# Values in three blocks per group in the first cross attention, and rotated halves formed from one projection in the second self attention

## Chip, cores and metric

The kernel runs on one core of one Trainium2 chip. The metric is the device time of one execution in microseconds (us); smaller is better. An execution is one launch that runs the whole two-layer decoder.

## The reference, cut to what matters

Two decoder layers, each of self attention, cross attention and a feed-forward part, with a layer norm after each. The change touches two of the six parts. The first is layer 0's cross attention, with 2048 queries, 1601 keys and 16 heads of 64:

```python
q = (x @ w_q).reshape(B, SQ, N_HEADS, D_HEAD)
k = (cond @ w_k).reshape(B, SKV, N_HEADS, D_HEAD)
v = (cond @ w_v).reshape(B, SKV, N_HEADS, D_HEAD)
attn = softmax(einsum('bqhd,bkhd->bhqk', q, k) * scale)
out = einsum('bhqk,bkhd->bqhd', attn, v).reshape(B, SQ, N_HEADS * D_HEAD)
return out @ w_out + b_out
```

The second is layer 1's self attention, causal, with 2 heads of 128. Of each head's 128 features the first 64 are rotated by position and the others stay as they are:

```python
even, odd = split(rot, 2, axis=-1)          # 32 features each
r_even = even * cos - odd * sin
r_odd = even * sin + odd * cos
return concatenate([r_even, r_odd, skip], axis=-1)
```

## The kernel before

The parts of the decoder run one after another. Within a part each engine has its own written-out list of instructions, in an order set at build time, and semaphores tie the lists together. An engine never takes its list out of order.

**The first cross attention** (`l0_cross_heads`) works in 32 groups: 8 pairs of heads by 4 tiles of 512 queries. A group has 13 steps, `kt` 0 to 12, one for each 128 keys. In a step TensorE computes the scores of both heads, with the keys on the partitions (`scores`, L867: eight matmuls on 64 rows, so that the two heads lie in the two halves of the array), ScalarE takes the exponential (`exponentials`, L1032) into one of `NP` buffers `pr` (two of them lie in `o_nat`), GpSimd adds it to a running sum (L783, L779), and TensorE multiplies it with the values (`values`, L882: four matmuls of 128 rows by 64 columns for a step). Beside it runs work for later groups. 32 maxima per group, for the group after next or thereabouts: TensorE computes a piece of 400 scores of one head (L823, also on 64 rows), and VectorE reduces it (L921); after the last of a group VectorE takes the least of the pieces (L928), TensorE turns it (L829, "shift"), VectorE copies it (L936), and a DMA puts it in place. Then the projections `q` and `k`, the sum of the exponentials over partitions (`sum`, L835), the output projection (`out`, L845).

These side units share three banks of PSUM, `pM`, in turn. The unit with number n may start on TensorE when the unit n-3 has been emptied: a maximum by VectorE's reduction, `out` by VectorE's addition (L971), `q` and `k` by VectorE's subtraction (L915) after a copy on ScalarE (L1011), `sum` by ScalarE (L1018). VectorE also makes four reciprocals per group (L943, after the maxima of steps 5 to 8) and the normalised output (L950, after those of step 9). `units_in(g, kt)` says which units a step has, 2 or 3 maxima and then the others. `values` run at the end of steps 0, 1, 3, 5, 7, 9 and 11, for one or two steps at a time.

**The second self attention** (`l1_self_attention`) works in 8 items x: 4 tiles of 512 positions by 2 heads. Each item needs q and k rotated. The rotation's swapped halves come from a second projection with columns swapped in the weights (`qs`, `ks`), so that there are four projections per item (L1735, four matmuls each). VectorE multiplies the straight one with cos (L1878), the swapped one with sin (L1887) and adds (L1891); ScalarE rounds the sum to its high part (L2017), and VectorE subtracts for the low part (L1870). Again units share three banks. `project(x + 2)` is laid out during item x: its first two units, then `shift` of item x + 1 (L1771, copied by VectorE in L1914), then the rest. The scores of item x + 1 (L1823) wait for that copy. In items 1 and 2 VectorE also normalises rows of the experts' output (L1955 to L1967) before its first unit, and in items 3 and 5 it takes statistics (L1939, L1941) there.

Of the kernel before, what the change touches and what calls it, by code (L numbers as in the profile page):

```python
# [13 lines left out]
P = 128  # L14
T = 2048
# [595 lines left out]
def l0_cross_heads(nc, A, G, sems):  # L611
# [9 lines left out]
    NP = 4  # L621
# [38 lines left out]
    last = [("out", GROUPS - 2, 1), ("sum", GROUPS - 1), ("out", GROUPS - 1, 0), ("out", GROUPS - 1, 1)]  # L660
# [4 lines left out]
    with ExitStack() as ctx:  # L665
# [11 lines left out]
        unit_rows = m.sb("x0unit", [P, P], F32R)  # L677
        kept = G.o_nat[:, :, :].rearrange("p c n -> p (c n)").bitcast(F32).rearrange("p (b a q) -> p b a q", b=2, a=2)
        pr = [kept[:, 0, :, :], kept[:, 1, :, :]] + [m.sb(f"x0pr{i}", [P, 2, QG])[:, :, :] for i in range(2)]
# [5 lines left out]
        rc = m.sb("x0rc", [P, QG])  # L685
        oc = m.sb("x0oc", [P, QG])
# [38 lines left out]
        with nc.Block() as block:  # L725
            @block.sync
            def _(sp):
# [22 lines left out]
                sp.wait_ge(s_set, 4)  # L750
# [8 lines left out]
            def _(pool):  # L759
                for i in range(2):  # L760
                    nc.gpsimd.memset(sh[i][:, :].bitcast(F32), 0.0).then_inc(s_set, 1)
                nc.gpsimd.memset(unit_rows[:, :].bitcast(F32), 0.0).then_inc(s_set, 1)
                pool.wait_ge(s_set, 3)
                nc.gpsimd.memset(unit_rows[0:1, :].bitcast(F32), 1.0).then_inc(s_set, 1)
                pool.wait_ge(s_set, 4)
                nc.gpsimd.memset(unit_rows[64:65, :].bitcast(F32), 1.0).then_inc(s_set, 1)
                pool.wait_ge(s_set, 5)
# [19 lines left out]
            def _(pe_):  # L787
# [98 lines left out]
                pe_.wait_ge(s_set, 5)  # L886
# [12 lines left out]
                values(STEPS - 2)  # L899
                values(STEPS - 1)  # L900
# [4 lines left out]
            def _(dve):  # L905
# [32 lines left out]
                def reciprocals(g, i):  # L938
                    wait_emptied(dve, ("sum", g))
                    if i == 0 and g >= 1:  # L940
                        dve.wait_ge(s_on, g)
                    c = slice(i * P, (i + 1) * P)
                    nc.vector.reciprocal(rc[:, c], dn[:, c]).then_inc(s_rc, 1)  # L943

                def normalise(g):
                    dve.wait_ge(s_rc, 4 * (g + 1))
                    dve.wait_ge(s_oc, g + 1)
                    if g >= 2:
                        wait_filled(dve, ("out", g - 2, 1))
                    nc.vector.tensor_tensor(on[g % 2][:, :], oc[:, :], rc[:, :], ALU.mult).then_inc(s_on, 1)  # L950
# [40 lines left out]
                unit(last[0])  # L991
                for i in range(4):
                    reciprocals(GROUPS - 1, i)
                normalise(GROUPS - 1)
                for name in last[2:]:
                    unit(name)

            @block.scalar
            def _(act):
# [13 lines left out]
                def sums(name):  # L1013
                    g = name[1]
                    wait_filled(act, name)
                    if g >= 1:
                        act.wait_ge(s_rc, 4 * g)
                    emptied(nc.scalar.activation(dn[:, :], bank(name)[:, :], ACT.Copy), name)  # L1018

                def copy_out(g):  # L1020
                    act.wait_ge(s_pv, NK * (g + 1))
                    if g >= 1:
                        act.wait_ge(s_on, g)
                    nc.scalar.activation(oc[:, :], pO[:, :], ACT.Copy).then_inc(s_oc, 1)
# [527 lines left out]
def l1_self_attention(nc, A, G, sems, acc_d):  # L1552
# [50 lines left out]
    with ExitStack() as ctx:  # L1603
        m = Mem(nc, ctx, sems)
        cos, sin = m.sb("a1cos", [P, T]), m.sb("a1sin", [P, T])
        w = [m.sb(f"a1w{h}", [P, DJ, 4, HD]) for h in range(H)]
# [6 lines left out]
        ta, tb = [m.sb(f"a1ta{i}", [P, QG]) for i in range(2)], m.sb("a1tb", [P, QG])  # L1613
# [23 lines left out]
        s_add, s_hi, s_lo = m.sem("a1_rotated"), m.sem("a1_high"), m.sem("a1_low")  # L1637
# [10 lines left out]
        def emptied(ins, name):  # L1648
            ins.then_inc(s_free[number[name] % 3], 1)
# [18 lines left out]
        with nc.Block() as block:  # L1668
# [57 lines left out]
            def _(pe_):  # L1726
                def rotated(name):
                    kind, x = name
                    g, h = x // H, x % H
                    part = {"q": 0, "qs": 1, "k": 2, "ks": 3}[kind]  # L1730
# [72 lines left out]
                def unit(name):  # L1803
                    if number[name] >= 3:
                        pe_.wait_ge(s_free[number[name] % 3], number[name] // 3)
                    {"q": rotated, "qs": rotated, "k": rotated, "ks": rotated, "v": value_rows, "max": maximum,
# [56 lines left out]
            def _(dve):  # L1863
# [9 lines left out]
                def straight(name):  # L1873
# [9 lines left out]
                def swapped(name):  # L1883
                    kind, x = name[0][0], name[1]
                    wait_filled(dve, name)
                    here = slice((x // H) * QG, (x // H + 1) * QG)
                    emptied(nc.vector.tensor_tensor(tb[:, :], bank(name)[:, :], sin[:, here], ALU.mult), name)  # L1887
                    wait_emptied(dve, (kind, x))
                    wait_emptied(dve, name)
                    mine = ta["qk".index(kind)][:, :]  # L1890
                    nc.vector.tensor_tensor(mine, mine, tb[:, :], ALU.add).then_inc(s_add, 1)  # L1891
# [86 lines left out]
                def unit(name):  # L1978
                    if name[0] not in ("v", "x", "z"):
                        {"q": straight, "qs": swapped, "k": straight, "ks": swapped, "max": maximum, "shift": shifts,  # L1980
# [28 lines left out]
            def _(act):  # L2009
                def high(name):  # L2010
                    kind, x = name[0][0], name[1]
# [20 lines left out]
                def unit(name):  # L2032
                    if name[0] in ("qs", "ks"):
# [826 lines left out]
def rotary_tables():  # L2860
# [5 lines left out]
            np.concatenate([-s, s, np.zeros((64, T), np.float32)]))  # L2866


def layout(i):

    ac = np.ascontiguousarray
    swap = np.concatenate([np.arange(32, 64), np.arange(0, 32), np.arange(64, 128)])
# [13 lines left out]
        "a1_w": np.stack([a1["wq"].reshape(D, D), a1["wq"][:, :, swap].reshape(D, D),  # L2886
                          a1["wk"].reshape(D, D), a1["wk"][:, :, swap].reshape(D, D)]),
# [28 lines left out]
```

## Time and profile before

| | us |
|---|---|
| median of 3 executions | 3599.84 (3599.75 to 3606.65) |
| profiled execution, its own time | 3592.38 |
| its span in the profile | 3590.6 |
| its granted TensorE clock | 0.952 of full speed |

The profiled execution's own time is 1.8 us more than its span. The profile shows the busy time of each engine (PE is TensorE, PEld its weight loads, DVE VectorE, ACT ScalarE, POOL GpSimd), and gives times in us from the span's start. A matmul's record is longer than the time it holds the array, since matmuls overlap; what it holds is read from the distance between starts.

### The profile page before, as it was taken

The numbers are of one execution on the slowest core, as the hardware profiler recorded it, in microseconds if no ns is written. First come the engines' busy times: TensorE is split into PE (matmuls) and PEld (weight loads), VectorE is DVE, ScalarE is ACT, GpSimd is POOL, SyncE is SP. The second block draws the span as 40 slices with busy tenths as digits, with TensorE's granted clock in tenths as the row PEclk, the third lists the DMA queues.
The fourth block names the chain that finished last, engine by engine and source line by source line (L and its number), as shares of the span: only waits on it lengthen the run. The fifth ranks groups of instructions, "written<-read, shape, count | busy, mean of one in ns | idle before, by whom it ended". The sixth has DMA issues, their size and how long they took to land. (4 is left out here: it accounts for less than half of the span.)

```text
span 3590.6 us, 60640 instructions
## 1 busy us (share of the span) xinstructions
PE 3201.4 (89%) x22601; PEld 1809.7 (50%) x22601; DVE 2355.7 (66%) x5271; ACT 1721.9 (48%) x2086; POOL 1711.3 (48%) x1145
## 2 busy tenths in 40 slices
PE   6899999989999999999999817689979989999787
PEld 3666666644555555555555407655544333333346
DVE  3999999945656656656656481264427878888528
ACT  1788888833444344444344322222224656666641
POOL 2888888824767777777778702212350000000012
PEclk9999999999999999999999958889977999999999
DMA  2000000020000000000000066500021111111001
GB/s 71 25 2 2 2 2 2 2 53 1 4 1 3 4 1 4 1 4 1 4 1 1 1 197 202 151 13 1 1 42 17 17 17 17 17 17 17 18 14 36
DMA packets 62572, 88.14 MB, mean 25 GB/s; under 512 B 9458, under 2 KB 52339, under 8 KB 61427
## 3 DMA queue, kind: packets, MB, share of 16 engines
q1 hardware_dynamic: 59250, 80.27, 9.2%
q0 software_dynamic: 3072, 4.34, 0.7%
q8 instruction: 182, 2.98, 0.4%
q14 instruction: 68, 0.55, 0.0%
HBM read 61.28 MB, written 8.54 MB: 19 GB/s over the span
## 5 line engine op out<-in xcount | busy, mean ns | idle before, releaser
L921 DVE TENSOR_REDUCE x0hm<-x0pM 128x1 f32<-128x400 f32 (+1 forms) x1024 | 520.2, 561 | 379.7 <-PE x0pM L823 379.7
L402 POOL TENSOR_SCALAR rows<-rows,mb 128x1024 bf16<-128x1024 bf16 x512 | 567.4, 1119 | 131.2 <-DVE mb L354 131.2
L348 DVE TENSOR_SCALAR_CACHE_REDUCE rows<-pS 128x1024 bf16<-128x1024 f32 x512 | 616.4, 1205 | 19.0 <-PE pS L297 19.0
L413 ACT ACTIVATE prT<-pP 128x1024 bf16<-128x1024 bf16 x512 | 523.3, 1024 | 134.4 <-PE pP L308 133.9
L1381 DVE TENSOR_REDUCE x1hm<-x1pM 128x1 f32<-128x400 f32 (+1 forms) x1024 | 512.6, 564 | 112.3 <-PE x1pM L1273 112.2
L1500 ACT ACTIVATE x1pr<-x1pST 128x1024 f32<-128x1024 f32 (+1 forms) x416 | 419.2, 1023 | 218.3 <-PE x1pST L1325 208.1
L783 POOL TENSOR_TENSOR x0acc<-x0acc,x0pr 128x1024 f32<-128x1024 f32 (+1 forms) x176 | 421.4, 2395 | 111.1 <-ACT x0pr L1032 95.3
L783 POOL TENSOR_TENSOR x0acc<-x0acc,o_nat 128x1024 f32<-128x1024 f32 (+1 forms) x176 | 418.9, 2380 | 71.9 <-ACT o_nat L1032 53.1
L1273 PE MATMUL x1pM<-x1sk,x1sq 64*128 64x400 f32 (+1 forms) x1024 | 361.2, 451 | 58.4 <-DVE x1hm L1381 29.4
L2590 POOL MEMSET f_tri<- 128x128 f32 x1 | 0.2, 209 | 730.2 <-POOLq L1179 730.2
L1032 ACT ACTIVATE o_nat<-x0pST 128x1024 f32<-128x1024 f32 (+1 forms) x208 | 213.0, 1024 | 279.8 <-PE x0pST L867 279.6
L1032 ACT ACTIVATE x0pr<-x0pST 128x1024 f32<-128x1024 f32 (+1 forms) x208 | 212.9, 1024 | 279.4 <-PE x0pST L867 279.4
L1273 PEld LDWEIGHTS x1pM<-x1sk,x1sq 64*128 64x128 f32 x1024 | 163.0, 192 | 336.2 <-issue 163.5
L308 PE MATMUL pP<-ident_b,rows 128*128 128x128 bf16 x4096 | 318.4, 221 | 0.9 <-ACT prT L413 0.5
L823 PE MATMUL x0pM<-x0kh,x0qh 64*128 64x400 f32 (+1 forms) x1024 | 280.0, 369 | 11.2 <-ACT x0v L1042 4.0
L308 PEld LDWEIGHTS pP<-ident_b,rows 128*128 128x128 bf16 x4096 | 230.8, 98 | 116.4 <-issue 58.3
L297 PE MATMUL pS<-kT,qT 64*128 64x512 bf16 x1024 | 201.4, 390 | 74.9 <-PEq L136 18.8
L1325 PE MATMUL x1pST<-x1sq,x1sk 64*128 64x512 f32 (+1 forms) x832 | 224.3, 426 | 6.0 <-DMA x1sq<-x1nt 3.8
L1339 PE MATMUL x1pO<-x1pr,x1v 128*32 128x512 f32 (+1 forms) x1664 | 223.3, 609 | 0.5 <-ACT x1pr L1500 0.4
L867 PE MATMUL x0pST<-x0qh,x0kh 64*128 64x512 f32 (+1 forms) x832 | 223.3, 449 | 0.0
L882 PE MATMUL x0pO<-x0pr,x0v 128*64 128x512 f32 (+1 forms) x832 | 210.8, 604 | 0.1
L882 PE MATMUL x0pO<-o_nat,x0v 128*64 128x512 f32 (+1 forms) x832 | 210.6, 604 | 0.0
(362 smaller groups left out, 5127.2 us busy)
## 6 DMA issues: line engine op xcount, KB each, us to landing
m_w<-in_moe_w1T SPq DMA_DIRECT2D x16, 1024.0 KB, 9.8
m_w<-in_moe_w2T SPq DMA_DIRECT2D x16, 1024.0 KB, 6.3
x1sq<-x1qh SPq DMA_DIRECT2D x32, 128.0 KB, 4.4
x1sk<-x1kh SPq DMA_DIRECT2D x32, 100.1 KB, 3.6
rows_d<-m_xr SPq DMA_DIRECT2D x1, 2176.0 KB, 7.8
acc_d<-m_zero SPq DMA_DIRECT2D x4, 514.0 KB, 7.4
m_acc<-acc_d SPq DMA_DIRECT2D x4, 514.0 KB, 6.8
g_xN<-in_x SPq DMA_DIRECT2D x1, 2048.0 KB, 8.8
```

Source lines behind the costliest of these rows:

```text
L308: mm = nc.tensor.transpose(pP[half][:, k, :], rows[u][:, kt * P:(kt + 1) * P], G.ident_b[:, :])
L348: nc.vector.tensor_scalar(rows[u][:, half * 1024:(half + 1) * 1024], pS[half][:, :], 1.0, None, ALU.mult, ALU.max, accum_out=mx[u][:, half ...
L402: nc.gpsimd.tensor_scalar(r, r, -1.0, mb[u][:, 0:1], ALU.mult, ALU.add).then_inc(s_df, 1)
L413: nc.scalar.activation(prT[u][:, half * 8:(half + 1) * 8, :], pP[half][:, :, :], ACT.Exp, scale=-1.0 / HD ** 0.5).then_inc(s_ex, 1)
L783: nc.gpsimd.tensor_tensor(total[0:r, :, :], total[0:r, :, :], pr[n % NP][0:r, :, :], ALU.add)\
L823: filled(nc.tensor.matmul(bank(name)[:, 0:w], qh[g % 3][half, t * P:(t + 1) * P], kh[g // 4 % 2][half, c0:c0 + w], start=True, stop=True), ...
L882: mm = nc.tensor.matmul(pO[64 * a:64 * a + 64, :], v_all[0:r, kt, c:c + HD], pr[n % NP][0:r, a, :], start=(kt == 0), stop=(kt == NK - 1))
L921: emptied(nc.vector.tensor_reduce(hm[g % 2][:, a, t, i % 8 // 2:i % 8 // 2 + 1], bank(name)[:, 0:w], AX.X, ALU.max, negate=True), name)
L1032: nc.scalar.activation(pr[n % NP][0:r, :, :], pST[n % 2][0:r, :, :], ACT.Exp, scale=HD ** -0.5)\
L1273: filled(nc.tensor.matmul(bank(name)[:, 0:w], q[part, c:c + P], k[part, c0:c0 + w], start=True, stop=True), name)
L1381: emptied(nc.vector.tensor_reduce(hm[u % 2][:, a, t, i % 8 // 2:i % 8 // 2 + 1], bank(name)[:, 0:w], AX.X, ALU.max, negate=True), name)
L1500: nc.scalar.activation(pr[step % 3][0:r, g::2, :], pST[n % 2][0:r, :, :], ACT.Exp, scale=HD ** -0.5).then_inc(s_ex, 1)
```

## The change

In the first cross attention the values of a group run in three blocks, at the end of steps 4, 8 and 0 of the next group, for 4, 4 and 5 steps. The other units move to the same three steps: `sum` and `q` to step 4, both `k` to step 8, both `out` to step 0. There are six buffers of exponentials for four. The reciprocals overwrite their input and the normalisation works in place; two buffers go. The rows of ones for the shift come from a constant that is there already, so that three GpSimd fills go.

In the second self attention there are two projections per item, `q` and `k`. VectorE forms the swapped halves with two multiplications of 32 partitions each, which read the bank at other partitions than they write, and the addition covers 64 partitions. A bank is free after three VectorE operations. Since `project(x + 2)` now has only two units (except where `z` leads it), `shift` of item x + 1 comes behind both of them in odd items. The weights and the sine table loaded are half as large.

```diff
-    NP = 4
+    NP = 6
...
-        if kt == 1 and g + 2 < GROUPS:
+        if kt == 0 and g >= 2:
+            units += [("out", g - 2, 0), ("out", g - 2, 1)]
+        if kt == 4 and g >= 1:
+            units.append(("sum", g - 1))
+        if kt == 4 and g + 2 < GROUPS:
             units.append(("q", g + 2))
-        if kt == 3 and g >= 1:
-            units.append(("sum", g - 1))
-        if kt == 11 and g >= 1:
-            units.append(("out", g - 1, 0))
-        if kt == 0 and g >= 2:
-            units.append(("out", g - 2, 1))
-        if g // 4 + 1 < H // 2 and g % 4 < 2 and kt in (5, 9):
-            units.append(("k", g // 4 + 1, 2 * (g % 4) + kt // 9))
+        if kt == 8 and g // 4 + 1 < H // 2 and g % 4 < 2:
+            units += [("k", g // 4 + 1, 2 * (g % 4)), ("k", g // 4 + 1, 2 * (g % 4) + 1)]
         return units
+
+    def values_in(n):
+
+        kt = n % NK
+        if kt in (4, 8):
+            return range(n - 4, n)
+        return range(n - 5, n) if n and kt == 0 else ()
...
-        unit_rows = m.sb("x0unit", [P, P], F32R)
+        unit_rows = G.ones[:, :].bitcast(F32R)
...
-                    if kt == 1:
-                        values(n - 1)
-                    elif n and kt % 2 == 1 or n and kt == 0:
-                        values(n - 2)
-                        values(n - 1)
-                values(STEPS - 2)
-                values(STEPS - 1)
+                    for k in values_in(n):
+                        values(k)
+                for k in values_in(STEPS):
+                    values(k)
...
-                    nc.vector.reciprocal(rc[:, c], dn[:, c]).then_inc(s_rc, 1)
+                    nc.vector.reciprocal(dn[:, c], dn[:, c]).then_inc(s_rc, 1)
...
-                    nc.vector.tensor_tensor(on[g % 2][:, :], oc[:, :], rc[:, :], ALU.mult).then_inc(s_on, 1)
+                    nc.vector.tensor_tensor(on[g % 2][:, :], on[g % 2][:, :], dn[:, :], ALU.mult).then_inc(s_on, 1)
...
-        units = [(k, x) for k in ("q", "qs", "k", "ks")]
+        units = [("q", x), ("k", x)]
...
-                def straight(name):
+                def rotated(name):
                     kind, x = name
                     wait_filled(dve, name)
                     dve.wait_ge(s_rot[x // H], 32)
                     here = slice((x // H) * QG, (x // H + 1) * QG)
-                    emptied(nc.vector.tensor_tensor(ta["qk".index(kind)][:, :], bank(name)[:, :], cos[:, here], ALU.mult),
-                            name)
+                    upper, lower = slice(0, HD // 4), slice(HD // 4, HD // 2)
+                    mine, swapped = ta["qk".index(kind)], tb["qk".index(kind)]
+                    nc.vector.tensor_tensor(mine[:, :], bank(name)[:, :], cos[:, here], ALU.mult).then_inc(s_cos, 1)
+                    nc.vector.tensor_tensor(swapped[upper, :], bank(name)[lower, :], sin[lower, here], ALU.mult)\
+                        .then_inc(s_sin, 1)
+                    emptied(nc.vector.tensor_tensor(swapped[lower, :], bank(name)[upper, :], sin[upper, here], ALU.mult), name)
                     if kind == "k":
                         low("q", x)
...
+                    dve.wait_ge(s_cos, done)
+                    dve.wait_ge(s_sin, done)
                     wait_emptied(dve, name)
...
+                    both = slice(0, HD // 2)
+                    nc.vector.tensor_tensor(mine[both, :], mine[both, :], swapped[both, :], ALU.add).then_inc(s_add, 1)
                     if kind == "k":
                         low("k", x)
```

## Rows read from the trace of the kernel before

**Rows 1.** Windows: start:end, length, busy us (instructions) by engine, clock, DMA; both parts.

```profile
core 0: us, PE busy (x) PEld busy (x) DVE busy (x) ACT busy (x) POOL busy (x), PEclk, DMA share, GB/s
840.00:2062.00 1222.00, 1200.14 (x6617) 636.16 (x6616) 722.57 (x1338) 494.86 (x538) 915.93 (x384) 0.99 0.01 2
2318.24:2642.30 324.06, 291.15 (x1064) 167.29 (x1064) 147.84 (x333) 83.11 (x125) 80.81 (x79) 0.92 0.06 18
```

**Rows 2.** Timeline of PE, cross attention: start us, length us, line, what it writes and reads.

```profile
1003.79 0.53 PE L823 MATMUL x0pM<-x0kh,x0qh 64*128 64x400 f32 x3
1003.97 0.58 PE L867 MATMUL x0pST<-x0qh,x0kh 64*128 64x512 f32 x2
...
1012.05 0.45 PE L823 MATMUL x0pM<-x0kh,x0qh 64*128 64x400 f32 x1
1012.42 0.65 PE L882 MATMUL x0pO<-o_nat,x0v 128*64 128x512 f32 x2
...
1012.91 0.59 PE L882 MATMUL x0pO<-o_nat,x0v 128*64 128x512 f32 x1
1013.33 0.60 PE L882 MATMUL x0pO<-x0pr,x0v 128*64 128x512 f32 x2
...
1013.76 0.60 PE L882 MATMUL x0pO<-x0pr,x0v 128*64 128x512 f32 x2
1014.29 0.50 PE L867 MATMUL x0pST<-x0qh,x0kh 64*128 64x512 f32 x2
1014.63 0.40 PE L867 MATMUL x0pST<-x0qh,x0kl 64*128 64x512 f32 x2
1014.86 0.39 PE L867 MATMUL x0pST<-x0ql,x0kh 64*128 64x512 f32 x2
```

**Rows 3.** Timeline of DVE, cross attention; in brackets the idle time before and its releaser.

```profile
1012.13 0.57 DVE L921 TENSOR_REDUCE x0hm<-x0pM 128x1 f32<-128x402 f32 x1
1012.61 0.94 DVE L943 RECIPROCAL x0rc<-x0dn 128x128 f32<-128x128 f32 x1
1013.47 0.99 DVE L921 TENSOR_REDUCE x0hm<-x0pM 128x1 f32<-128x402 f32 x2
...
1151.71 2.50 DVE L921 TENSOR_REDUCE x0hm<-x0pM 128x1 f32<-128x400 f32 x5 [0.93 <-PE x0pM L823]
```

**Rows 4.** Timeline of DVE: the normalised output of two groups that follow each other.

```profile
1097.02 0.97 DVE L950 TENSOR_TENSOR x0on<-x0oc,x0rc 128x512 f32<-128x512 f32 x1
...
1133.69 0.97 DVE L950 TENSOR_TENSOR x0on<-x0oc,x0rc 128x512 f32<-128x512 f32 x1
```

**Rows 5.** Timeline of PE: the sum of the last group, with what it waited for.

```profile
2051.61 1.98 PE L835 MATMUL x0pM<-x0acc,ones 128*64 128x512 f32 x4 [4.70 <-POOL x0acc L783]
```

**Rows 6.** Groups by line of the second self attention: xcount, busy us, mean ns, idle before.

```profile
L1735 PE MATMUL a1pM<-g_xT,a1w 128*128 128x512 f32 x128 | 60.8, 622 | 1.6 <-ACT g_xT L2029 1.6
```

**Rows 7.** Timeline of item 1's rotation, from its first projection to the first scores.

```profile
2349.19 0.69 DVE L1878 TENSOR_TENSOR a1ta<-a1pM,a1cos 128x512 f32<-128x512 f32 x1 [0.68 <-PE a1pM L1735]
...
2352.63 0.69 DVE L1878 TENSOR_TENSOR a1ta<-a1pM,a1cos 128x512 f32<-128x512 f32 x1 [0.23 <-PE a1pM L1735]
2353.23 0.68 DVE L1870 TENSOR_TENSOR a1ql<-a1ta,a1qh 128x512 fp32r<-128x512 f32 x1
...
2357.13 0.67 DVE L1914 CAST a1shift<-a1pM 1x512 bf16<-1x512 f32 x1
...
2357.95 0.47 PE L1823 MATMUL a1pST<-a1qh,a1kh 128*128 128x512 f32 x1 [3.33 <-DVE a1shift L1914]
```

**Rows 8.** Timeline of PE: a wait in item 2, then the last two steps of item 3.

```profile
2412.32 0.47 PE L1759 MATMUL a1pM<-a1kh,a1qh 128*128 128x128 f32 x1 [5.63 <-DVE a1hm L1900]
...
2461.10 1.88 PE L1735 MATMUL a1pM<-g_xT,a1w 128*128 128x512 f32 x4
2462.42 0.68 PE L1823 MATMUL a1pST<-a1qh,a1kh 128*128 128x256 f32 x1
...
2465.99 1.88 PE L1735 MATMUL a1pM<-g_xT,a1w 128*128 128x512 f32 x4
...
2472.44 0.48 PE L1823 MATMUL a1pST<-a1qh,a1kh 128*128 128x512 f32 x1
```

More of the change, by code:

```diff
@@ L659, in l0_cross_heads @@
     number, count = {}, 0
-    last = [("out", GROUPS - 2, 1), ("sum", GROUPS - 1), ("out", GROUPS - 1, 0), ("out", GROUPS - 1, 1)]
+    last = [("out", GROUPS - 2, 0), ("out", GROUPS - 2, 1), ("sum", GROUPS - 1), ("out", GROUPS - 1, 0), ("out", GROUPS - 1, 1)]
     for name in first + [n for g in range(GROUPS) for kt in range(NK) for n in units_in(g, kt)] + last:
@@ L676, in l0_cross_heads @@
         sh = [m.sb(f"x0sh{i}", [P, QG], F32R) for i in range(2)]
-        unit_rows = m.sb("x0unit", [P, P], F32R)
+        unit_rows = G.ones[:, :].bitcast(F32R)
         kept = G.o_nat[:, :, :].rearrange("p c n -> p (c n)").bitcast(F32).rearrange("p (b a q) -> p b a q", b=2, a=2)
-        pr = [kept[:, 0, :, :], kept[:, 1, :, :]] + [m.sb(f"x0pr{i}", [P, 2, QG])[:, :, :] for i in range(2)]
+        pr = [kept[:, 0, :, :], kept[:, 1, :, :]] + [m.sb(f"x0pr{i}", [P, 2, QG])[:, :, :] for i in range(NP - 2)]
         acc = [m.sb(f"x0acc{i}", [P, 2, QG]) for i in range(2)]
@@ L884, in values @@
                     mm.then_inc(s_pv, 1)
-                pe_.wait_ge(s_set, 5)
+                pe_.wait_ge(s_set, 2)
                 for name in first:
@@ L991, in _ @@
                 unit(last[0])
+                unit(last[1])
                 for i in range(4):
@@ L994, in _ @@
                 normalise(GROUPS - 1)
-                for name in last[2:]:
+                for name in last[3:]:
                     unit(name)
@@ L1021, in copy_out @@
                     act.wait_ge(s_pv, NK * (g + 1))
-                    if g >= 1:
-                        act.wait_ge(s_on, g)
-                    nc.scalar.activation(oc[:, :], pO[:, :], ACT.Copy).then_inc(s_oc, 1)
+                    if g >= 2:
+                        wait_filled(act, ("out", g - 2, 1))
+                    nc.scalar.activation(on[g % 2][:, :], pO[:, :], ACT.Copy).then_inc(s_oc, 1)
                 def exponentials(n):
@@ L1604, in l1_self_attention @@
         m = Mem(nc, ctx, sems)
-        cos, sin = m.sb("a1cos", [P, T]), m.sb("a1sin", [P, T])
-        w = [m.sb(f"a1w{h}", [P, DJ, 4, HD]) for h in range(H)]
+        cos, sin = m.sb("a1cos", [P, T]), m.sb("a1sin", [HD // 2, T])
+        w = [m.sb(f"a1w{h}", [P, DJ, 2, HD]) for h in range(H)]
         wv, wo = m.sb("a1wv", [P, DJ, D]), m.sb("a1wo", [P, H, D])
@@ L1612, in l1_self_attention @@
         kl = [m.sb(f"a1kl{h}", [P, T], F32R) for h in range(H)]
-        ta, tb = [m.sb(f"a1ta{i}", [P, QG]) for i in range(2)], m.sb("a1tb", [P, QG])
+        ta, tb = [m.sb(f"a1ta{i}", [P, QG]) for i in range(2)], [m.sb(f"a1tb{i}", [HD // 2, QG]) for i in range(2)]
         pr = [m.sb(f"a1pr{i}", [P, 2, QG]) for i in range(NP)]
@@ L1877, in straight @@
                     here = slice((x // H) * QG, (x // H + 1) * QG)
-                    emptied(nc.vector.tensor_tensor(ta["qk".index(kind)][:, :], bank(name)[:, :], cos[:, here], ALU.mult),
-                            name)
+                    upper, lower = slice(0, HD // 4), slice(HD // 4, HD // 2)
[4 more added lines that the diff above has]
+                    emptied(nc.vector.tensor_tensor(swapped[lower, :], bank(name)[upper, :], sin[upper, here], ALU.mult), name)
                     if kind == "k":
                         low("q", x)
[L1883 to L1888, printed above, removed]
+                    done = 2 * x + (1 if kind == "q" else 2)
+                    dve.wait_ge(s_cos, done)
+                    dve.wait_ge(s_sin, done)
                     wait_emptied(dve, name)
-                    mine = ta["qk".index(kind)][:, :]
-                    nc.vector.tensor_tensor(mine, mine, tb[:, :], ALU.add).then_inc(s_add, 1)
+                    both = slice(0, HD // 2)
+                    nc.vector.tensor_tensor(mine[both, :], mine[both, :], swapped[both, :], ALU.add).then_inc(s_add, 1)
                     if kind == "k":
@@ L1979, in unit @@
                     if name[0] not in ("v", "x", "z"):
-                        {"q": straight, "qs": swapped, "k": straight, "ks": swapped, "max": maximum, "shift": shifts,
+                        {"q": rotated, "k": rotated, "max": maximum, "shift": shifts,
                          "sum": total, "out": out}[name[0]](name)
@@ L2010, in high @@
                 def high(name):
-                    kind, x = name[0][0], name[1]
+                    kind, x = name
                     g, h = x // H, x % H
@@ L2032, in unit @@
                 def unit(name):
-                    if name[0] in ("qs", "ks"):
+                    if name[0] in ("q", "k"):
                         high(name)
```

29 lines of the change are left out of this document (8 added, 21 removed).

## The prediction

> **What bounds the kernel.** I read the windows first. The cross attention takes 1222 us of the span with PE busy for 98% of it, DVE for 59% and POOL for 75%; the second self attention takes 324 us with PE at 90% [rows 1]. By these shares both are PE's. But a busy PE can also be one whose matmuls stand in line behind a wait, so I read the timeline next, by distances between starts.
>
> What the cross attention's units hold of PE [rows 2]: a round of scores 0.23 us (1014.63 to 1014.86), so 0.93 for the four of a step; a maximum 0.09, since two heads' maxima share 0.18 (three start at 1003.79, the next score at 1003.97); a pair of value matmuls 0.42 (1012.91 to 1013.33), so 0.85 a step. A projection, `sum` or two `out` takes four such slots of 0.43, 1.7 us (`sum` and one `out` half of it).
>
> Going to the values and back costs something each way [rows 2]. In: last maximum to first value 0.37 where 0.17 would do, and the first pair takes 0.49 for 0.42. Out: last pair to first score 0.53 for 0.43, first round 0.34 for 0.23. Together 0.20 + 0.06 + 0.10 + 0.11, some 0.45 us a visit. A shorter sum without stalls, for a group with no `k` unit: scores 12.1, maxima 2.8, values 11.0, `q` 1.7, `out` 1.7, `sum` 0.9, seven visits 3.2, the side units inside them and the shift 0.8. That is 34.2 us. Such a group takes 36.67 (1097.02 to 1133.69) [rows 4]. So some 2.5 us per group are waits that PE's busy share hides, and they are waits for VectorE: it empties the three banks at one maximum per 0.48 us (five in 2.50, the last 0.56 long) [rows 3], against 0.09 on PE.
>
> **Part one, the values in three blocks.** Removed: four of seven visits, 4 x 0.45 = 1.8 us per group. Side units keep their work; entering them beside values costs about the same before and after (`out` twice together saves a switch, `sum` followed by `q` adds one). If nothing else moved, 32 groups would give 58 us.
>
> What else moves is where VectorE can work. It has per group 32 maxima (15.4 us), four reciprocals at 0.86 (1012.61 to 1013.47), a normalisation of 1.0, and copies and additions [rows 3, 4]: some 23 of 37 us, enough time overall. But PE may lead it by three banks only. While PE multiplies values it feeds VectorE nothing: at most three maxima wait, 1.4 us of work, and today's block of two steps (1.7 us) just covers that. A block of four or five lasts 3.4 to 4.2 us, longer with `q`, `k` or `out`, and VectorE idles the rest. Afterwards it must do in one run all maxima between two blocks, with the reciprocals, whose places in its list stay at steps 5 to 8. I walk each run from its first score. The first maximum can be reduced after 1.03 (first score, switch included) + 0.34 (matmul) + 0.04 = 1.4 us; PE leaves the run when the unit three banks back is emptied (0.08 after its slot, 0.06 to restart).
>
> - Steps 1 to 4, then `sum`: PE alone 4 x 0.93 + 0.10 + 10 x 0.09 + 0.1 = 4.8 us. `sum` needs the eighth of ten maxima emptied: 1.4 + 8 x 0.48 + 0.14 = 5.4, and two short idle times of VectorE make 5.6. Loss 0.8.
> - Steps 5 to 8, with three reciprocals in the way, the group minimum (0.10) and the shift's copy (0.2): 1.4 + (2 + 3 + 2 + 1) x 0.48 + 3 x 0.86 + 0.3 + 0.14 = 8.3, with idle time 8.5. PE alone 5.2, shift included. Loss 3.3. Before, the same reciprocals lay beside values at the ends of steps 5 and 7.
> - Steps 9 to 0, with the normalisation: `out` needs the tenth of twelve: 1.4 + 10 x 0.48 + 1.0 + 0.14 = 7.3. PE alone 5 x 0.93 + 0.10 + 12 x 0.09 + 0.1 = 5.9. Loss 1.4.
>
> Losses 5.5 for today's 2.5, less 1.8 saved: +1.2 us per group. Groups 1 to 29 have both: 29 x 1.2 = 35. Group 0 has no reciprocals and comes out some 1.6 ahead, group 30 has half the maxima, about 1.0 ahead. The last group has none, but its end is not PE's: `sum` waits 4.70 us for POOL's additions [rows 5], which start with the exponentials and not with the values; I take nothing. Cross attention **+32 us**.
>
> Bounds: if the losses stay at today's 2.5, -58; if each run of VectorE's is 0.25 us longer than walked, 32 + 32 x 0.75 = +56. I take the walk, because every term of it has a row.
>
> The Trainium skill (TensorEngine Tiling (Array Packing), Key Properties) says that a change of tiling mode drains the engine. The 0.45 us per visit in the trace agree; by that rule alone the change is worth the 58 us. The same page (Performance Considerations, PSUM Bottleneck) says that tiling makes TensorE faster and not the emptying of PSUM, so that the copy out may become the limit. That speaks against this change, and the 0.48 against 0.09 us in the trace agree.
>
> Six buffers for four free ScalarE sooner, which waits for nothing there: 0. In the place of the fills there is a constant; their place is GpSimd's start, before PE's projections: 0 to -1, taken as 0. In-place operations have the same shapes: 0. POOL's additions, 12 x 2.4 = 29 us of a group's 37 (75% busy [rows 1]), are late at no step: with six buffers an exponential waits for an addition six steps back. If that cover were gone, a late addition would hold exponentials, then scores.
>
> **Part two, one projection.** Removed: 64 of 128 matmuls. They hold 60.8 / 128 = 0.475 us of PE each in union [rows 6], 0.43 warm, so 27.5 us if all were on the path; that and 0 are the bounds of its gain. VectorE has 3 operations where it had 2 before the addition, at 0.60 each from start to start (2352.63 to 2353.23) [rows 7]; an operation on 32 partitions is not in the trace, and by its 512 elements per partition I take the same 0.60 (bounds 0.3 and 0.7, 1.6 us and less over 16 units).
>
> What is on the path is the chain of one item's rotation. From q's bank to scores it takes 8.76 us now (2349.19 to 2357.95) [rows 7]. With both banks there early: q's three multiplications 2.0 and addition 0.6; k's three 1.8, low of q 0.6, addition 0.75, rounding 0.66, low of k 0.6, shift copy and start 0.8: 7.8 us. So it is 0.95 shorter, not two projections (3.4) shorter. By item:
> - 0: the first maximum follows the chain; PE saves two slow projections, half of it is given back waiting: -2.8.
> - 1: -0.95. 2: VectorE does the experts' rows right after, and PE then waits for it anyway: -0.9. 3: the same, the wait of 5.63 is there now [rows 8]: -0.8.
> - 4: even item, shift ahead of the projections, which now lie together behind the steps; the statistics of VectorE come first: -2.2 of 3.4. 6: the same, one projection earlier before: -3.4.
> - 5: shift is now behind both. Before, q's projection at 2461.10 and step 2462.42 to 2465.99 (3.57), then three projections, scores at 2472.44 [rows 8]. After: 2461.10 + 3.57, q full 1.95 later, chain 7.8: 2474.4. **+2.0**. 7: half the chain after the move, +0.8.
>
> Sum -8 us. Smaller loads end before the first projection anyway: 0.
>
> **Sum.** The profiled execution's own time is 3592.4, 1.8 over its span; the runs' median is 3599.8, 7.4 above it. 3592.4 + 32 - 8 = 3616.4; by the median, 3599.8 + 24 = **3624 us**.
>
> **Rivals.**
> - *The visits are all that counts.* If VectorE catches up inside the longer blocks, the cross attention gives its 58 us and the self attention 8: 3600 - 66 = 3534. For it: PE's 98% busy, VectorE's 59%. Against: three banks hold 1.4 us of work, the block lasts 3.4. It decides where the losses per group are below 2.5 + 1.8 = 4.3 us for my 5.5; the reciprocals' 2.6 us in one run are what tips it. By the skill's rule on draining it would be so. Chance 0.10, and 0.03 for something between it and no change on the fast side.
> - *The self attention gives all 27 us* because its waits dissolve: 3600 + 32 - 27 = 3605, +0.14%. For it: PE 90% busy there. Against: the chain of rows 7. With cross losses a little under the walk, too. Chance 0.10.
> - *Waits lower the clock.* The granted clock is 0.99 in the cross attention and 0.92 in the self attention, where PE waits more [rows 1]. If one run in each group, 8 us, went at half speed for half of its 5 us of matmuls, 2.5 x 32 = +80: 3704. PE's waits there stay near 1 us each, shorter than the 5.63 of rows 8. Chance 0.05.
> - *Forecast*, 3606 to 3652: 0.72.
>
> No change is what a measurement of this kernel can't tell from 0.2%, 7 us. Slower 0.79, same 0.08, faster 0.13. The range for 8 in 10 goes from 3596 (cross +15, self -19) to 3652 (cross +56, self -4).
>
> **What would show it.** Profile after: values in starts of 8 or 10 pairs; L882 busy less, PE's share in the cross attention down from 98% to some 93%, with idle time before L823 and L829 that names L921 and L943; distance of two L950 without `k` 36.7 to 37.9. Around steps 5 to 8 VectorE without idle time for about 7 us, then idle in the block. In the self attention 64 records of L1735's line, and waits of 4 to 5 us before scores that name the shift's copy in items 4 and 6. I am wrong if the distance of L950 falls below 36, or if VectorE's reductions come closer than 0.48 us.

## The result: slower by 5.1%

| | before | after |
|---|---|---|
| median of the runs | 3599.8 us (3596.1 to 3606.7, 4 runs) | 3787.0 us (3774.0 to 3791.6, 4 runs) |
| ratio to before | 1 | 1.051 [1.048, 1.054] |
| profiled span | 3590.6 us | 3772.3 us |
| forecast | | 3624 us (3596 to 3652) |

The change makes the kernel slower, as forecast, but by 187 us where 24 were forecast. The windows of the profile after, of the same two parts as in [rows 1] (start:end, length, then busy us and instructions by engine, the granted clock and the DMA share):

```profile
854.10:2215.30 1361.20, 1243.46 (x6579) 679.31 (x6580) 768.19 (x1330) 493.60 (x535) 905.00 (x380) 0.93 0.01 2
2496.30:2821.60 325.30, 273.07 (x1000) 159.45 (x1000) 156.85 (x350) 82.49 (x125) 80.67 (x79) 0.88 0.06 15
```

The first is the cross attention from its first score matmul to its last; cut at the same two instructions, the profile of before has:

```profile
840.00:2043.70 1203.70, 1191.57 (x6595) 632.38 (x6596) 717.11 (x1331) 492.65 (x535) 908.60 (x381) 1.00 0.01 2
```

So 157.5 of the 181.7 us between the two spans are in this one stage. PE is now busy for 91% of it instead of 99% (forecast 93%), DVE has 51 us more of busy time for the same instructions, and the clock fell from 1.00 to 0.93. The second self attention took 325.3 us for 324.1. Of the rest, 14.1 us are in the head, ahead of the cross attention (854.1 against 840.0), which the change hardly touches; 6.5 lie between the two parts and 2.4 behind them.

The groups by line of the cross attention say what PE waits for. Before, its costliest group, the maxima, had 7.1 us of idle time in front of it. After:

```profile
L821 PE MATMUL x0pM<-x0kh,x0qh 64*128 64x400 f32 x978 | 291.9, 403 | 89.9 <-DVE x0hm L916 85.4
```

And here is where, in VectorE's and PE's timelines of one group (steps 5 to 8 first, then 9 and on):

```profile
1568.00 1.05 DVE L916 TENSOR_REDUCE x0hm<-x0pM 128x1 f32<-128x400 f32 x2 [3.49 <-PE x0pM L821]
1568.97 0.94 DVE L936 RECIPROCAL x0dn<-x0dn 128x128 f32<-128x128 f32 x1
1569.83 0.98 DVE L916 TENSOR_REDUCE x0hm<-x0pM 128x1 f32<-128x400 f32 x2
...
1574.68 1.03 DVE L916 TENSOR_REDUCE x0hm<-x0pM 128x1 f32<-128x400 f32 x2
...
1583.63 1.06 DVE L916 TENSOR_REDUCE x0hm<-x0pM 128x1 f32<-128x400 f32 x2 [2.64 <-PE x0pM L821]
1584.60 2.88 DVE L941 TENSOR_TENSOR x0on<-x0on,x0dn 128x512 f32<-128x512 f32 x1
1587.41 3.13 DVE L916 TENSOR_REDUCE x0hm<-x0pM 128x1 f32<-128x402 f32 x6
```

```profile
1566.59 0.50 PE L865 MATMUL x0pST<-x0qh,x0kh 64*128 64x512 f32 x2
...
1572.86 0.27 PE L827 MATMUL x0pM<-ident,x0nm 128*8 128x128 f32 x1 [0.62 <-DVE x0hm L916]
1573.34 0.45 PE L821 MATMUL x0pM<-x0kh,x0qh 64*128 64x400 f32 x1 [0.20 <-DVE x0hm L916]
1574.62 0.45 PE L821 MATMUL x0pM<-x0kh,x0qh 64*128 64x400 f32 x1 [0.84 <-DVE x0hm L916]
1575.00 3.70 PE L800 MATMUL x0pM<-x0ctxT,x0wk 96*128 96x512 f32 x8
...
1588.03 0.93 PE L821 MATMUL x0pM<-x0kh,x0qh 64*128 64x400 f32 x2 [1.91 <-DVE x0hm L916]
```

The run of steps 5 to 8 goes as walked: from the first score (1566.59) to the next unit, `k` (1575.00), 8.41 us, where the walk had 8.5. VectorE works from 1568.00 to 1575.71 without a break. But the normalisation, L941, takes 2.88 us, where the walk had 1.0 and [rows 4] show 0.97, and PE's longest wait of the group, 1.91 us, is for the maximum behind it. It does so in 29 of the 32 groups (the last three take 0.69 to 0.74). The trace's answer on this line for six groups in a row (duration in ns: least, median, most; first and last start), after and, for the same six groups, before:

```profile
L941 DVE TENSOR_TENSOR x0on<-x0on,x0dn x6: 2869/2874/2884, 1456.1 to 1673.1; 128x512 f32<-128x512 f32 x6
```

```profile
L950 DVE TENSOR_TENSOR x0on<-x0oc,x0rc x6: 669/964/1162, 1366.5 to 1557.0; 128x512 f32<-128x512 f32 x6
```

Five distances in 217.0 us are 43.4 us from one normalisation to the next, where the same five took 38.1 before (190.5 us). Two of the five are groups with `k` units. Without `k` the distance is now 41.0 to 44.0 us, where the forecast had 36.7 to 37.9.

### The profile page after: what moved, and what is told of

It is laid out like the page before. It is cut to its first block and busy times, and to the rows that moved or that the text cites. A ratio compares the mean times of both kernels' runs of the same rounds, so it can differ in the third digit from the quotient of the medians.

```text
span 3772.3 us, 60459 instructions
## 1 busy us (share of the span) xinstructions
PE 3243.0 (86%) x22537; PEld 1852.6 (49%) x22537; DVE 2431.0 (64%) x5287; ACT 1722.1 (46%) x2086; POOL 1709.7 (45%) x1142
## 5 line engine op out<-in xcount | busy, mean ns | idle before, releaser
L781 POOL TENSOR_TENSOR x0acc<-x0acc,x0pr 128x1024 f32<-128x1024 f32 (+1 forms) x235 | 559.9, 2383 | 173.9 <-ACT x0pr L1024 146.2
L1024 ACT ACTIVATE x0pr<-x0pST 128x1024 f32<-128x1024 f32 (+1 forms) x276 | 282.5, 1025 | 368.6 <-PE x0pST L865 359.8
L821 PE MATMUL x0pM<-x0kh,x0qh 64*128 64x400 f32 (+1 forms) x1024 | 306.1, 405 | 94.1 <-DVE x0hm L916 85.4
L781 POOL TENSOR_TENSOR x0acc<-x0acc,o_nat 128x1024 f32<-128x1024 f32 (+1 forms) x117 | 279.2, 2386 | 87.2 <-ACT o_nat L1024 73.5
L821 PEld LDWEIGHTS x0pM<-x0kh,x0qh 64*128 64x128 f32 x1024 | 171.1, 198 | 217.2 <-DVE x0hm L916 178.5
L880 PE MATMUL x0pO<-x0pr,x0v 128*64 128x512 f32 (+1 forms) x1104 | 275.4, 628 | 0.0
L865 PE MATMUL x0pST<-x0qh,x0kh 64*128 64x512 f32 (+1 forms) x832 | 240.3, 457 | 1.0 <-ACT x0pr L1024 0.8
L1024 ACT ACTIVATE o_nat<-x0pST 128x1024 f32<-128x1024 f32 (+1 forms) x140 | 143.3, 1025 | 184.0 <-PE x0pST L865 179.8
```

The source lines that it names most:

```text
L781: nc.gpsimd.tensor_tensor(total[0:r, :, :], total[0:r, :, :], pr[n % NP][0:r, :, :], ALU.add)\
L821: filled(nc.tensor.matmul(bank(name)[:, 0:w], qh[g % 3][half, t * P:(t + 1) * P], kh[g // 4 % 2][half, c0:c0 + w], start=True, stop=True), ...
L880: mm = nc.tensor.matmul(pO[64 * a:64 * a + 64, :], v_all[0:r, kt, c:c + HD], pr[n % NP][0:r, a, :], start=(kt == 0), stop=(kt == NK - 1))
L1024: nc.scalar.activation(pr[n % NP][0:r, :, :], pST[n % 2][0:r, :, :], ACT.Exp, scale=HD ** -0.5)\
```

## The experiments

The experiments had three theories. *The runs of VectorE*: the prediction's walk, +32 us. *The normalisation*: at its new place it meets an addition of GpSimd, +1.9 us per group. *The clock*: PE's waits bring the lower level of its clock (1.2 GHz, for 2.4 at full speed), and everything of PE then takes longer. Ratios are to the kernel before on the same chip, with 95% intervals.

**self_only and cross_only.** Each half of the change alone, on the kernel before.

> The kernel before with the second self attention of the change alone. By the chain of one item's rotation (shorter by 0.95 us, and behind it two items whose scores wait for the shift's copy) it gains 8 us: 3592. By matmuls alone it gains 27 us: 3573. If the waits it adds let the clock fall, it gains nothing: 3600, with more time at the low clock in that part.

> The kernel before with the first cross attention of the change alone. If all of the loss is there, 3600 + 160 to 185 us. The cross attention of the changed kernel took 1361 us from first to last score, of before 1204: the same 1361 is expected here, with the normalisation 2.88 us long and about 44 stretches at the low clock.

Measured: self_only 3617.3 us, ratio 1.003 [1.001, 1.005]; cross_only 3781.0, 1.048 [1.044, 1.053], as expected. The self attention's half is worth nothing or a few us, on the slow side, where its expectations had a gain or nothing; the loss is the cross attention's.

**rec_in_block.** The four reciprocals go behind the maxima of step 4, and the normalisation behind those of step 8, so that VectorE does both while PE multiplies values.

```diff
-                    if g and 5 <= kt < 9:
-                        reciprocals(g - 1, kt - 5)
-                    elif g and kt == 9:
+                    if g and kt == 4:
+                        for i in range(4):
+                            reciprocals(g - 1, i)
+                    elif g and kt == 8:
```

> The changed kernel, with VectorE's four reciprocals right after the maxima of step 4 and the normalisation after those of step 8, both where TensorE is in a block of values. By my walk the run of steps 5 to 8 loses 2.6 us of reciprocals and the run of steps 9 to 0 the whole normalisation (1.0 us by its own work, 2.9 with its wait for GpSimd): some 5.5 us less per group at full clock, 30 x 5.5 = 165, and most of the low clock gone: 3787 - 165 to 240 = 3550 to 3620. If the loss came from the block length itself (drains, buffers, GpSimd late), less than 40 us of it comes back: above 3745.

Measured: 3556.5 us, 0.986 [0.982, 0.990]. From 5% slower to 1.4% faster by two places in VectorE's list. The cross attention, 1361 us after and 1204 before, takes 1146; PE is busy for 99% of it, at full clock:

```profile
857.10:2003.50 1146.40, 1130.44 (x6579) 634.12 (x6580) 720.50 (x1330) 493.37 (x536) 906.48 (x380) 1.00 0.01 2
```

**norm_in_block and rec_only.** The two moves one by one. The edit shown is norm_in_block's; rec_only has rec_in_block's reciprocals, with the normalisation where after has it.

```diff
-                    elif g and kt == 9:
+                    if g and kt == 8:
```

> The changed kernel with only the normalisation moved, from after the maxima of step 9 to after the last reciprocal of step 8, in a block of values. If its 2.9 us there are what my walk lacked, 2.9 us less per group, 87 us, plus what the clock gives back: 3787 - 87 to 130 = 3655 to 3700. If the reciprocals in one run are the whole loss, 0 to 30 us: above 3755.

> The changed kernel with only the four reciprocals moved, to right after the maxima of step 4; the normalisation stays after step 9. By my walk with a normalisation of 2.88 us the run of steps 5 to 8 loses 2.4 us less per group: 72 us at full clock, and most of the 180 us at the low clock gone, worth 0.43 us each: 3787 - 72 - 50 = 3665, between 3640 and 3695, with the normalisation still 2.88 us long. If the normalisation's wait alone had been the loss, above 3755.

Measured: norm_in_block 3654.0 us, 1.014 [1.010, 1.018], at the edge of what was expected; rec_only 3614.2, 1.001 [0.999, 1.003]. Neither move alone beats before; both together do. In norm_in_block 17 of the 32 normalisations still take 2.5 to 2.75 us, but now while PE multiplies values, where their length costs PE nothing: steps 9 to 0 take the same 6.7 us there as in rec_in_block, for 9.3 to 10.5 in after. rec_only came out below what was expected of it. The trace says why: the normalisation stayed at its place, but not all of them take long there. Five in a row, shortest, median and longest:

```profile
L941 DVE TENSOR_TENSOR x0on<-x0on,x0dn x5: 683/722/2876, 1113.2 to 1266.4; 128x512 f32<-128x512 f32 x5
```

So the 2.88 us are not the instruction's own; they depend on what it meets.

**half_sum.** What it meets is GpSimd. Its timeline of after, in the stretch shown above:

```profile
1568.92 7.36 POOL L781 TENSOR_TENSOR x0acc<-x0acc,x0pr 128x1024 f32<-128x1024 f32 x3 [2.35 <-ACT x0pr L1024]
1576.43 2.35 POOL L781 TENSOR_TENSOR x0acc<-x0acc,o_nat 128x1024 f32<-128x1024 f32 x1
1584.56 2.38 POOL L781 TENSOR_TENSOR x0acc<-x0acc,o_nat 128x1024 f32<-128x1024 f32 x1 [5.78 <-ACT o_nat L1024]
1587.08 5.16 POOL L781 TENSOR_TENSOR x0acc<-x0acc,x0pr 128x1024 f32<-128x1024 f32 x2
```

The addition starts at 1584.56, the normalisation 0.04 us later; the addition ends at 1586.94, the normalisation at 1587.48, 0.54 later. The kernel before has the same tie, which the prediction did not read. At 1133.69 [rows 4] the normalisation starts in the second of two additions that end at 1134.11 and ends at 1134.66; at 2004.89 it starts 0.56 us behind one:

```profile
1129.22 4.89 POOL L783 TENSOR_TENSOR x0acc<-x0acc,x0pr 128x1024 f32<-128x1024 f32 x2
1134.25 2.67 POOL L783 TENSOR_TENSOR x0acc<-x0acc,o_nat 128x1024 f32<-128x1024 f32 x1
...
2004.33 2.38 POOL L783 TENSOR_TENSOR x0acc<-x0acc,o_nat 128x1024 f32<-128x1024 f32 x1 [0.41 <-ACT o_nat L1032]
2004.89 2.37 DVE L950 TENSOR_TENSOR x0on<-x0oc,x0rc 128x512 f32<-128x512 f32 x1
```

The traces of all twelve kernels hold 384 normalisations. 356 start while an addition runs, and each of them ends 0.55 to 0.67 us after it; the other 28 take 0.69 us. So the 0.97 of [rows 4] was itself 0.69 and a wait of 0.28, and the same instruction took 0.67 to 2.37 us before. It works the other way too: the addition at 1134.25, which starts while the normalisation runs, takes 2.67 us instead of 2.3 to 2.4.

half_sum makes the additions of steps 2 to 12 half as long; it leaves out the second head's sum of exponentials from step 2 on.

```diff
-    nc.gpsimd.tensor_tensor(total[0:r, :, :], total[0:r, :, :], pr[n % NP][0:r, :, :], ALU.add)
+    nc.gpsimd.tensor_tensor(total[0:r, 0, :], total[0:r, 0, :], pr[n % NP][0:r, 0, :], ALU.add)
```

> The changed kernel with GpSimd's additions of steps 2 to 12 made for the first head of the pair only (512 elements per partition for 1024): the second head's sum of exponentials is left out from step 2 on. If the normalisation waits for the end of GpSimd's addition, it becomes as much shorter as that addition: 2.88 - 1.15 = 1.7 us, 1.1 us per group, 35 to 60 us with the clock: 3727 to 3752. If the 2.88 us come from its operands (in place, two from SBUF), its length stays 2.88 and the time above 3770.

Measured: 3707.4 us, 1.027 [1.024, 1.031]. The normalisation's length follows the addition's, in VectorE's and GpSimd's timelines and over six groups:

```profile
1595.08 1.78 DVE L941 TENSOR_TENSOR x0on<-x0on,x0dn 128x512 f32<-128x512 f32 x1
...
1595.03 4.39 POOL L781 TENSOR_TENSOR x0acc<-x0acc,x0pr 128x512 f32<-128x512 f32 x3 [11.91 <-ACT x0pr L1024]
```

```profile
L941 DVE TENSOR_TENSOR x0on<-x0on,x0dn x6: 1780/1796/1815, 1465.8 to 1674.5; 128x512 f32<-128x512 f32 x6
```

The kernel gained more than was expected (3727 to 3752 us) and more than the 1.1 us per group of the shorter normalisation: the cross attention fell by 58.1 us to 1303.1, and by 1.1 x 31 = 34 it would be 1327. The other 24 us are put down to the clock, which rose from 0.93 to 0.96 there, with 85 us less at the lower level (95.1 for 180.5): 0.28 us for each.

**double_max.** The theory of the clock, by filling PE's waits: after's kernel with each score matmul of a maximum issued twice.

```diff
-                    filled(nc.tensor.matmul(bank(name)[:, 0:w], qh[g % 3][half, t * P:(t + 1) * P],
-                                            kh[g // 4 % 2][half, c0:c0 + w], start=True, stop=True), name)
+                    for twice in range(2):
+                        mm = nc.tensor.matmul(bank(name)[:, 0:w], qh[g % 3][half, t * P:(t + 1) * P],
+                                              kh[g // 4 % 2][half, c0:c0 + w], start=True, stop=True)
+                    filled(mm, name)
```

> After's kernel, with each score matmul of a maximum issued twice into the same bank (the same values, so the output is unchanged): 2.8 us more of TensorE's work per group of the first cross attention, 90 us in 32 groups, put where TensorE waits for VectorE. If TensorE's waits are what lowered the clock in the first cross attention (180 us at the lower level there), most of that time goes back to the higher level, worth up to 77 us, and at most 30 us of the added work shows: 3710 to 3745. If the low clock has nothing to do with the waits, nothing is given back and 30 to 90 us are added: 3815 to 3875.

Measured: 3761.1 us, 1.044 [1.042, 1.046], 26 us less than after, with some 1000 matmuls more. The windows, the whole cross attention and one of four groups in it:

```profile
858.10:2202.20 1344.10, 1252.78 (x7555) 746.04 (x7553) 768.14 (x1330) 493.21 (x535) 907.60 (x380) 0.98 0.01 2
...
1793.50:1964.10 170.60, 158.50 (x968) 94.39 (x964) 100.26 (x173) 62.40 (x69) 114.86 (x49) 1.00 0.01 2
```

The clock went from 0.93 to 0.98 in the stage. Neither expectation held by its numbers: it lies between the two, nearer to the clock's. Added up from the records of the granted clock, time at 1.2 GHz fell from 180.5 us to 40.9. At the price worked out below, 0.43 to 0.47 us per us, that gives 60 to 66 back, and the stage gained 17; so 43 to 49 us of the added work showed, 1.4 to 1.5 per group, where at most 30 us were expected (at half_sum's 0.28 it would be 39 back and 22 shown). That filled waits raise the clock is shown; the balance was mis-sized.

**rec_old_self and rec_shift_first.** rec_in_block's cross attention with the self attention of before, and with the new one in which `shift` of item x + 1 comes ahead of its projections again in odd items.

```diff
-        units = units + ahead[:2]
+        lead = [name for name in ahead if name[0] == "z"]
+        units = units + lead
...
-        units = units + ahead[2:]
+        units = units + ahead[len(lead):]
```

> The kernel with reciprocals and normalisation in the blocks (3556), with the second self attention as it was before the change. self_only was 0.3% slower than before, so that this one should be 3 to 11 us faster: 3545 to 3553. If the new self attention is worth its 8 us and the difference was chance, 3564.

> The kernel with reciprocals and normalisation in the blocks (3556), with the shift of the next item ahead of q and k in odd items too, in the new self attention. If the scores of items 2, 4 and 6 wait for the shift's copy behind the rotation, this gives 3.4 us for item 4, 2 to 3 for item 6 and 1 for item 2, and of the 85 us at the low clock some 30 come back at 0.43 each: 3556 - 7 - 13 = 3536, between 3530 and 3547. If the chain through VectorE and ScalarE holds the item's maxima anyway, under 3 us: above 3552.

Measured: rec_old_self 3556.7 us, 0.985 [0.982, 0.987], between its two expectations; rec_shift_first 3541.9, 0.982 [0.979, 0.985], as expected. With rec_in_block's 3556.5 (0.986) beside it, the new self attention as it stands is worth nothing, and by its window it even costs 3.6 us (327.7 against 324.1). With `shift` first its window is 318.8:

```profile
2269.70:2588.50 318.80, 270.93 (x1000) 157.68 (x1000) 157.27 (x349) 82.06 (x125) 80.60 (x79) 0.89 0.06 15
```

rec_shift_first beats both kernels. Of its lead over rec_in_block in the profiled pair, 16.7 us are the head, the time ahead of the cross attention (840.4 against 857.1 us), which the next run looks at.

**head_first.** rec_shift_first, with GpSimd's fills of the q tiles (sixteen) behind VectorE's first two convolution operations.

```diff
+                    pool.wait_ge(s_tap, 2)
                     for c in range(16):
                         nc.gpsimd.memset(qT[:, c, :].bitcast(F32), 0.0).then_inc(s_zero, 1)
```

> rec_shift_first's kernel, with POOL's eight fills of the q tiles (L162) behind a wait for VectorE's first two conv operations. In before's profile these two took 2.5 us each, in seven of the nine other kernels' profiles 18.8 to 19.1 us, with POOL filling beside them. If the fills are what holds them, the head is the short one in every execution: the median goes from 3541.9 to 3525 to 3540, with a narrower spread. Rival: the fills end some 6 us later and the transfers that wait for them start later, so that nothing comes of it, or up to 5 us more.

Measured: 3539.9 us (3539.3 to 3550.9), 0.982 [0.981, 0.984]: no gain over rec_shift_first that can be told. Four of its five executions lie within 2.5 us, and the profiled one is the slowest, 9 us above them. In that one the stall had only moved to the next pair (VectorE's timeline):

```profile
5.42 0.88 DVE L173 TENSOR_SCALAR xc<-xp,cw 128x512 f32<-128x512 f32 x2 [5.42 <-DMA cw<-in_conv]
6.22 2.73 DVE L178 SCALAR_TENSOR_TENSOR xc<-xp,cw,xc 128x512 f32<-128x512 f32 x4
9.52 19.06 DVE L173 TENSOR_SCALAR xc<-xp,cw 128x512 f32<-128x512 f32 x2 [0.56 <-DMA xp<-in_xT]
```

## Why the prediction was right in sign and wrong in size

**The visits' price and the walk of VectorE's runs held, to within some 13 us.** Steps 1 to 4 up to `sum` took 5.73 us in the trace of after (1554.35 to 1560.08; walked 5.6), steps 5 to 8 took 8.41 (walked 8.5). Steps 9 to 0 up to `out` took 9.34 in the five groups that ran them at full clock: walked 7.3, and 9.2 with the normalisation at its measured length. rec_in_block gives the counter-proof: when the reciprocals and the normalisation leave the runs, the longer blocks pay, 57 us in the cross attention. The same walk without their 2.6 and 1.0 us gives 2.4 us less per group, 70 in 29 groups; its runs of steps 5 to 8 and 9 to 0 took 6.15 and 6.68 us. So "the visits are all that counts" was wrong for the change as made, and nearly right once VectorE's work lies inside the blocks. The +32 us were not measured by themselves; no run speaks against them by more than those 13.

**The first step that failed is a term of that walk, the 1.0 in "1.4 + 10 x 0.48 + 1.0 + 0.14 = 7.3" for steps 9 to 0.** It came from [rows 4], where the instruction took 0.97 us. At its new place it takes 2.88, in 29 of 32 groups. Why always: GpSimd's addition there waits for the exponential of step 9's scores, and the normalisation stands behind the first maxima of the same step. Both are tied to the same restart of PE after the values, so that in those 29 groups they start within 0.05 us of each other; no slack lies between. The normalisation then ends 0.54 us after the addition. half_sum shows the dependence (1.79 us for an addition of half the size), rec_only that it is the meeting and not the place in the list (0.69 or 2.87), and the 384 normalisations of the twelve kernels leave no exception. 2.88 - 1.0 = 1.9 us per group; in the walk, 55 us in all.

The Trainium skill (SBUF — State Buffer, "Who interferes with whom") says that a VectorE instruction with two SBUF inputs contends with a GpSimd instruction that reads SBUF, calls the port pair that the two share an exclusive lock, and says that the order of issue decides who blocks. The traces agree: the normalisation reads two SBUF tiles, and the addition reads SBUF and is a hair ahead. The maxima, which read PSUM, keep their 0.48 us beside the same additions, and the reciprocals, which read one SBUF tile, their 0.94 (1568.97, in GpSimd's 7.36 us from 1568.92 on). The prediction counted additions only for being late and not for what they hold.

**The second step that failed is the clock, which the sum left out.** The rival "waits lower the clock" was given a chance of 0.05; its +80 us was the right size. The price of time at 1.2 GHz can be read at two places. cross_only and after have the same code in the stage and took 1377.4 and 1361.2 us, with 217.8 and 180.5 us at the lower level by the clock's records: 16.2 / 37.3 = 0.43 us per us. Within after, two windows of four groups each:

```profile
1102.90:1284.00 181.10, 165.46 (x838) 89.39 (x836) 100.76 (x173) 62.44 (x68) 114.41 (x49) 0.90 0.01 2
1284.00:1456.10 172.10, 156.46 (x839) 85.83 (x836) 100.31 (x174) 62.57 (x69) 114.56 (x49) 0.95 0.01 2
```

The same work at 0.90 and at 0.95 differs by 9.0 us. Between the two levels a mean of 0.90 is a fifth of the time at the lower one, 0.95 a tenth: 36 and 17 us, so 9.0 / 19 = 0.47. Before, the stage had 3.1 us at the lower level, after 180.5: 177 us more, worth 76 to 83 (50 by the 0.28 that half_sum leaves). The argument against the rival was that waits would stay near 1 us. The kernels put side by side say what the waits did (PE idle is the window less PE's busy time, the last column is added up from the clock's records):

| cross attention of | length, us | PE idle, us | at 1.2 GHz, us |
|---|---|---|---|
| before | 1203.7 | 12.1 | 3.1 |
| rec_in_block | 1146.4 | 16.0 | 2.9 |
| rec_only | 1196.2 | 41.3 | 29.9 |
| norm_in_block | 1244.1 | 62.1 | 71.1 |
| half_sum | 1303.1 | 87.0 | 95.1 |
| double_max | 1344.1 | 91.3 | 40.9 |
| after | 1361.2 | 117.7 | 180.5 |
| cross_only | 1377.4 | 117.6 | 217.8 |

norm_in_block has waits of 0.2 to 0.8 us alone (but for one of 2.1), and 71 us at the lower level: the 1.9 us behind the normalisation was not needed for part of it. double_max shows that the low clock belongs to the waits and is not a thing of its own. cross_only and after have the same waits and differ by 37 us at the lower level, so how much a given wait brings is not fixed.

**The sum.** 32 + 55 + 76 to 83 = 163 to 170 us, measured 157.5; with 50 for the clock, 137. The parts were not measured apart from each other to better than this, and how the 157.5 are shared out between them is open to some 20 us. The experiments stand in the same order. norm_in_block has a clock of 0.97 and rec_in_block of 1.00, and the stage is 40 us longer and 57 us shorter than before. The sign came out right, but mostly by two effects that the forecast did not have: of the 163 to 170 us, 131 to 138 are the wait for GpSimd and the clock.

**The self attention: -8 forecast, 1 to 4 us more measured.** The chain of item 1's rotation (VectorE's and PE's timeline of after):

```profile
2524.93 0.69 DVE L1872 TENSOR_TENSOR a1ta<-a1pM,a1cos 128x512 f32<-128x512 f32 x1 [0.68 <-PE a1pM L1727]
2525.66 0.68 DVE L1873 TENSOR_TENSOR a1tb<-a1pM,a1sin 32x512 f32<-32x512 f32 x1
2526.37 0.68 DVE L1875 TENSOR_TENSOR a1tb<-a1pM,a1sin 32x512 f32<-32x512 f32 x1
2527.18 0.68 DVE L1883 TENSOR_TENSOR a1ta<-a1ta,a1tb 64x512 f32<-64x512 f32 x1
...
2533.33 0.77 PE L1815 MATMUL a1pST<-a1qh,a1kh 128*128 128x512 f32 x1 [6.40 <-DVE a1shift L1906]
```

From q's bank to scores 8.40 us (2524.93 to 2533.33), where [rows 7] have 8.76 and the forecast 7.8. An operation on 32 partitions costs 0.71 from start to start (2525.66 to 2526.37), where 0.60 was taken; q's three multiplications take 2.25 for the 2.0 of the forecast (2524.93 to 2527.18), and k's are of the same make. The 64 records of L1727's line hold 32.0 us of PE, for 60.8 in [rows 6], so the projections did go, but their time turned into waits: 6.40 us here for 3.33 before. And the clock of the part fell from 0.92 to 0.88, in rec_in_block to 0.87; 0.05 x 2 x 327.7 = 33 us more at the lower level, some 14 us by the price of the cross attention (an estimate: it isn't measured here). By that estimate the new self attention would have gained about as forecast without the fall of the clock; no run shows it. The item that named the order of `shift` and projections was right in sign: with `shift` ahead the part is 8.9 us shorter than rec_in_block's, at a clock of 0.89 instead of 0.87, so part of it is the clock again.

## What to carry to other kernels

Price an instruction where it will stand, not where it stood, and read all its instances: one row said 0.97 us, the 32 of the same trace 0.67 to 2.37. Of each operation that is moved, ask which instruction of the other engines starts at that moment, and whether both hang on the same event, for then they collide every time and not now and then. When work of PE is bundled into longer blocks, move the other engine's long operations into the same blocks; here that alone turned 5.1% slower into 1.4% faster. And add to the price of any new wait of PE what its clock takes: here 0.3 to 0.5 us for each us at the lower level, in sum 50 to 83 us for 106 more of PE's idle time.

## What was not expected of the hardware

- *A lock in step.* A VectorE operation of 0.69 us takes 2.88 when it starts 0.04 us behind a GpSimd addition of 2.38, and 1.79 behind one of half the size. Its end follows the addition's by 0.55 to 0.67 us in 356 of 356 meetings.
- *Short waits lower the clock.* Waits of 0.2 to 1.9 us, five in a group of 43 us, brought 180 us at 1.2 GHz into a stage that had 3. More matmuls in the same waits brought it down to 41, and the kernel became 26 us faster with more work.
- *The first operation of the kernel is short or long, by chance.* VectorE's first pair of operations took 2.52 us in the profile of before, 2.40 in norm_in_block's, 1.66 in rec_shift_first's, and 18.7 to 19.1 in the eight others that left it at its place, after's among them. VectorE's timeline in before and in after:

```profile
5.37 2.52 DVE L172 TENSOR_SCALAR xc<-xp,cw 128x512 f32<-128x512 f32 x2 [5.37 <-DMA cw<-in_conv]
```

```profile
5.30 18.84 DVE L172 TENSOR_SCALAR xc<-xp,cw 128x512 f32<-128x512 f32 x2 [5.30 <-DMA cw<-in_conv]
...
1.63 14.57 POOL L162 MEMSET qT<- 128x1024 f32 x16
16.14 7.16 POOL L164 MEMSET kT<- 128x1024 f32 x8
```

The long one ends about when GpSimd's 24 fills do (23.30), and in head_first, where the fills end at 27.74, at 28.58. It costs the head some 14 us (854 to 858 us against 840 to 842). It is there with the old code too (in self_only the head and the cross attention are those of before), so 14 of the 182 us between the two profiled executions are most likely no effect of the change. That the fills hold the operation is what both ends suggest; what decides between the two lengths is open, and no version was run that keeps them apart throughout.
